# A last dense layer with low-rank adapters: split products and a masked adapter, or eight adapted weights and full-precision column halves

## What is computed

```python
x = x + einsum('bct,bcd->bdt', x, w0[cond])                   # mixing of the tokens, weight by batch
x = x + attention(x, block_table, kv_len)                     # 8 heads, 4 groups, window of 256, paged keys and values
x = x + einsum('bsi,bio->bso', x, W2[id]) + b2[id][:, None]   # one of 16 experts for each batch
H = einsum('btd,od->bto', x, W3)
delta = einsum('btr,bor->bto', einsum('btd,brd->btr', x, A[ad]), Bm[ad]) * scalings[ad]
x = x + H + delta                                             # ad: one of 8 adapters of rank 16 for each batch
```

## Time and profile before

| what | value |
|---|---|
| median of 3 runs | 1131.41 us (1126.84 to 1134.06) |
| profiled execution | 1129.37 us, span 1127.5 us, mean granted clock 0.969 |
| TensorE busy | 1043.9 us, 93% |
| VectorE, ScalarE, POOL busy | 659.9, 538.4, 534.1 us |
| phase 1 ends | at about 285 us |
| DMA | 196.16 MB, mean 174 GB/s |

### The profile page before, as it was taken

How to read it: one execution, slowest core, us unless ns; L and a number is a source line. 1 busy time by engine, 2 the same in 40 slices (tenths; PEclk the granted TensorE clock), 3 DMA queues, 4 the chain that set the end, 5 groups by cost and what they waited for, 6 DMA issues and landing times.

```text
span 1127.5 us, 23797 instructions
## 1 busy us (share of the span) xinstructions
PE 1043.9 (93%) x6418; PEld 704.5 (62%) x6418; DVE 659.9 (59%) x1928; ACT 538.4 (48%) x1337; POOL 534.1 (47%) x597
## 2 busy tenths in 40 slices
PE   7989999998579899999999999999999999999997
PEld 6767777676345566666666666666666666666655
DVE  5889896767345455555555555555554555555552
ACT  4457775674343444444444444444444444444440
POOL 3545444366555444545455545545454455454300
PEclk9999999999569899999999999999999999999998
DMA  4433443464367666575667666566765666566640
GB/s 131 143 117 135 150 153 116 161 194 139 92 180 209 178 186 200 184 218 178 181 193 219 207 187 211 185 185 181 220 209 182 187 214 186 175 201 214 194 147 20
DMA packets 95337, 196.16 MB, mean 174 GB/s; under 512 B 31346, under 2 KB 40114, under 8 KB 87110
## 3 DMA queue, kind: packets, MB, share of 16 engines
q1 hardware_dynamic: 63942, 149.49, 41.3%
q0 software_dynamic: 30784, 44.16, 14.3%
q10 hardware_dynamic: 576, 2.10, 0.5%
HBM read 195.08 MB, written 33.56 MB: 203 GB/s over the span
## 4 chain that ended last, share of the span: by engine, by line
PE 64%; issue 4%; ACT 3%; DMA 1%; another core or an unknown queue 1%; POOL 1%; DVE 1%; ACTq 0%; POOLq 0%; DVEq 0%
PE bank L93 23%; PE bank L1467 10%; PE bank L1442 9%; PE bank L1429 8%; PE bank L1421 8%; PE bank L1408 4%; PE bank L1398 2%; ACT PT L1227 2%; ACT KT L1227 1%; DMA KV<-kv_scratch,idxs 1%; DMA KV<-in_pool,idxs 1%; POOL KV L1129 0%; POOL KVE L1139 0%; DVE XB L1327 0%
## 5 line engine op out<-in xcount | busy, mean ns | idle before, releaser
L1227 ACT ACTIVATE PT<-bank 112x384 f32<-112x384 f32 x256 | 113.4, 489 | 254.4 <-PE bank L1429 211.6
L1305 DVE CUSTOM_DVE_ANT_0 SM<-bank,FM 128x336 f32<-128x336 f32 x256 | 129.7, 507 | 161.2 <-PE bank L1421 137.2
L1139 POOL DMA_INDIRECT KV<-kv_scratch,idxs x96 | 95.7, 997 | 127.2 <-DMA KV<-in_pool,idxs 103.9
L1139 POOL DMA_INDIRECT KVE<-kv_scratch,idxs_e x93 | 93.4, 1004 | 127.2 <-DMA KVE<-in_pool,idxs_e 102.5
L1236 ACT ACTIVATE PR<-SM,nb 128x336 f32<-128x336 f32 x256 | 145.5, 575 | 2.2 <-DVE nb L1309 2.1
L1129 POOL DMA_INDIRECT KV<-in_pool,idxs x96 | 95.1, 991 | 66.9 <-PE bank L1442 43.3
L1467 PE MATMUL bank<-W,XT 128*64 128x512 f32 x512 | 125.4, 612 | 0.7 <-ACT XT L1227 0.7
L1421 PE MATMUL bank<-KT,QB 64*128 64x336 f32 x512 | 111.2, 512 | 15.6 <-ACT KT L1227 8.8
L1227 ACT ACTIVATE KT<-bank 128x336 f32<-128x336 f32 x128 | 57.6, 450 | 141.2 <-PE bank L1408 134.8
L1129 POOL DMA_INDIRECT KVE<-in_pool,idxs_e x90 | 88.9, 988 | 70.8 <-PE bank L1442 42.7
L93 PE MATMUL bank<-wqh,XTH 128*128 128x512 f32 x256 | 105.2, 411 | 9.2 <-DVE XTL L500 5.8
(11 more groups left out here) (193 smaller groups left out, 2155.2 us busy)
## 6 DMA issues: line engine op xcount, KB each, us to landing
W<-in_w SPq DMA_DIRECT2D x64, 1024.0 KB
FM<-mask SPq DMA_DIRECT2D x64, 168.0 KB
X<-in_x SPq DMA_DIRECT2D x32, 256.0 KB
x_scratch<-X SPq DMA_DIRECT2D x32, 256.0 KB, 2.0
qt_scratch<-QT SPq DMA_DIRECT2D x32, 256.0 KB
QB<-qt_scratch SPq DMA_DIRECT2D x32, 256.0 KB
XB<-x_scratch SPq DMA_DIRECT2D x32, 256.0 KB
BB<-in_b SPq DMA_DIRECT2D x64, 128.0 KB
```

Source lines behind the costliest of these rows:

```text
L1139: pool.indirect_dma_start(out=KV[k][:, c, :], out_offset=None, in_=kv_d, in_offset=bass.IndirectOffsetOnAxis(ap=idxs[k][:, NCH + c:NCH + c ...
L1227: return nc.scalar.activation(dst, src, ACT.Copy)
L1305: v.tensor_tensor_reduce(out=SM[u % 2][:, :], in0=bank[u % 2][:, 0:SPAN], in1=FM[k][:, :], scale=1.0, scalar=-3e38, op0=ALU.add, op1=ALU.m ...
```

## The change

The eight possible weights of the last layer, W3 + scaling x (A Bm), are formed once and stay in SBUF (`W3E`, 128 x 16384 fp32). The last layer becomes eight fp32 matmuls of 64 stationary columns by 512, as the expert's are; the first batch of a pair reads its weight in W3E by an address from a register, the second reads a copy in `w3` that VectorE makes (`picked`). The split of the activations, the rank product and its mask go. On VectorE two slices are copied behind XO in front of `masked(pr, 4)`, two behind the bias addition in front of `masked(pr, 6)`.

- Forming: 32 steps (adapter, slice), each one float32r matmul with 48 contraction rows (high, low and high rows of A against high, high and low rows of Bm), to banks 6 and 7 in turn, and one VectorE scalar_tensor_tensor. 24 steps (`folded`, `products`) stand in pair 0 in eight places of three, on VectorE behind masked 1, masked 3, norm 1, masked 5, norm 2, masked 7 and two behind norm 3; 8 stand in pair 1 in two places of four.
- Late loads: W3 after pair 18 straight to `w3`, Wo after 23, A after 24, Bm after 27, the last two as 128 x 2048; six pieces of 1024 columns are split in place of five.
- XO lies over the phase 1 tile QT, XBB over XB3; VectorE waits in front of phase 2 for W3 and the last query store.

```diff
                 def late_low(i):
                     def run():
+                        part = slice(i % 2 * 1024, (i % 2 + 1) * 1024)
                         dve.wait_ge(s_wlh, i + 1)
-                        part = slice(i * 1024, (i + 1) * 1024)
-                        split(wlh[:, part], wll[:, part], wlr[:, part]).then_inc(s_wl, 1)
+                        if i < 2:
+                            split(woh[:, part], wol[:, part], wlr[:, part]).then_inc(s_wl, 1)
+                            return
+                        mixed, raw, neg = ((la, wlr[:, NWO:2 * NWO], nega), (lb, braw, negb))[i // 2 - 1]
+                        v.scalar_tensor_tensor(mixed[:, part], mixed[:, part].bitcast(F32), neg[:, 0:1], raw[:, part],
+                                               ALU.mult, ALU.add).then_inc(s_wl, 1)
...
-                                31: in_turn(late_low(3), late_low(4))})
+                                31: in_turn(late_low(3), late_low(4), late_low(5))})
...
+                    18: dense_weights, 23: output_weights, 24: adapter_inputs, 27: adapter_outputs})
...
                     if adapted:
                         act.wait_ge(s_x3p, at(r, 1, 0))
-                        copy(XTH3[:, :, :].rearrange("p k t -> p (k t)"), bank[7][:, :]).then_inc(s_xt3h, 1)
+                        copy(XT3[:, :, :, :].rearrange("p k b t -> p (k b t)"), bank[7][:, :]).then_inc(s_xt3, 1)
...
+                def adapted_weights(a, b):
+                    for i in range(a, b):
+                        ad, k = FOLDS[i]
+                        dve.wait_ge(s_low, i + 1)
+                        v.scalar_tensor_tensor(W3E[:, i * D:(i + 1) * D], bank[6 + i % 2][:, :], scb[:, ad:ad + 1],
+                                               w3[:, k, :], ALU.mult, ALU.add).then_inc(s_w3, 1)
+                def picked(q, ad, a, b):
+                    wait(dve, s_l3, q)
+                    for k in range(a, b):
+                        v.tensor_copy(w3[:, k, :], W3E[:, bass.ds(ad * (KC * D) + k * D, D)]).then_inc(s_w3c, 1)
...
                     if attention:
                         masked(pr, 0)
                         masked(pr, 1)
-                    if adapted:
-                        dve.wait_ge(s_xt3h, at(r, 1, 0))
-                        low(XTL3[:, :, :].rearrange("p k t -> p (k t)"), bank[7][:, :],
-                            XTH3[:, :, :].rearrange("p k t -> p (k t)")).then_inc(s_xt3, 1)
+                    if isinstance(p, int) and p == 1:
+                        adapted_weights(24, 24 + 4)
+                    folded(pr, 0)
...
+                        v.tensor_tensor(XO, bank[6][:, :], XB3[:, :], ALU.add).then_inc(s_xo, 1)
+                    if dense:
+                        ad = dve.value_load(aid[0:1, bass.ds(q * 2 + 1, 1)], min_val=0, max_val=NA - 1)
+                        picked(q, ad, 0, 2)
...
+                        v.tensor_tensor(XB3[:, :], XB2[:, :], BB[:, :], ALU.add).then_inc(s_xbb, 1)
+                        picked(q, ad, 2, KC)
 
                     if attention:
                         masked(pr, 6)
...
+                def dense3(r, ad, a, b):
+                    for k in range(a, b):
+                        pe.wait_ge(s_w3c, at(r, KC, k))
+                        for half in range(2):
+                            weight = w3[:, k, :] if half else W3E[:, bass.ds(ad * (KC * D) + k * D, D)]
+                            last = mm(bank[6][half * T:(half + 1) * T, :], XT3[:, k, half, :], weight,
+                                      start=(k == 0), stop=(k == KC - 1), skip_group_check=True)
+                    return last
+                def adapter_products(a, b):
+                    for i in range(a, b):
+                        ad, k = FOLDS[i]
+                        rows, g = slice(ad % 2 * T, ad % 2 * T + 3 * RANK), ad // 2 * D
+                        wait(pe, s_w3, i - 1)
+                        mm(bank[6 + i % 2][:, :], la[rows, g + k * P:g + (k + 1) * P], lb[rows, g:g + D], start=True,
+                           stop=True).then_inc(s_low, 1)
...
+                    if isinstance(p, int) and p == 1:
+                        adapter_products(24, 24 + 4)
                     if adapted:
+                        ad = pe.value_load(aid[0:1, bass.ds(r * 2, 1)], min_val=0, max_val=NA - 1)
                         pe.wait_ge(s_xt3, at(r, 1, 0))
-                        exact_products(mm, bank[7][:, 0:P], [(a_h[:, k, :], a_l[:, k, :], *x3t[k]) for k in range(KC)],
-                                       True, True).then_inc(s_xa, 1)
-                        dense3(0, 2, True)
+                        dense3(r, ad, 0, 2)
                     if attention:
                         scores(pr, 1)
+                        products(pr, 1)
                         turn(p, 0)
                         turn(p, 1)
+                    if isinstance(p, int) and p == 1:
+                        adapter_products(24 + 4, N_FOLDS)
+                        pe.wait_ge(s_w3, N_FOLDS)
                     if adapted:
-                        dense3(2, KC, False)
-                        pe.wait_ge(s_xal, at(r, 1, 0))
-                        exact_products(mm, bank[6][:, :], [(XAH[:, :], XAL[:, :], b_h[:, 0, :], b_l[:, 0, :])],
-                                       False, True).then_inc(s_l3, 1)
+                        dense3(r, ad, 2, KC).then_inc(s_l3, 1)
```

156 lines of the change are left out of this document (85 added, 71 removed).

## The result

The changed kernel takes 1146.86 us (median; 1141.51 to 1149.74), the kernel before 1132.74 on the same chip: ratio 1.0129, 95% interval 1.0081 to 1.0178. It is 1.3% slower, which is under 2% but clear of 1 by its interval; I had forecast 1114 us, a gain. The profiled execution took 1149.74 us, its span is 1147.9.

The account below looks back on a forecast made before the run. TensorE, busy 93% of the span, was taken as the bound; -49.0 + 18.6 + 0.5 + 14.5 - 2.5 = -17.9 us against the profiled 1129.37 gave 1111.5, 1114 us as a median, range 1088 to 1140.

Parts of the forecast that it names:

- TensorE's products: Steady loop: 5.18 us of products replaced by eight halves at 3.60, -1.58 us a pair, -49.0 us over 31 pairs.
- The register read: Steady loop: TensorE's read of the adapter number costs 0.6 us a pair, +18.6 us; bounds 0 and +38.
- A: Rival on the steady loop: register read hidden behind value products and dispatch lead, 1095 us; chance 0.25.
- C: Rival on the steady loop: TensorE also stops for address arithmetic before each register-addressed product, 1163 us; chance 0.17.
- Copies and VectorE: Steady loop: VectorE's four copies, 2.0 us a pair, fit its idle time and count nothing; uncovered, up to 31 us.
- Rival D: Steady loop: VectorE's SBUF copies hold up GpSimd's twelve gathers a pair, about 1245 us; chance 0.03.
- Phase change and first pairs: Late loads +0.5 us; forming in pairs 0 and 1 +14.5: pair 0 +6, pair 1 +7, lower clock +1.5.
- Tail: Last pair: eight halves at the lower clock replace 27 products, -2.5 us; bounds -1.7 and -5.3.
- The clock: Steady loop: granted clock taken to stay at its upper level, as TensorE's load hardly falls.
- The step that failed: Steady loop: GpSimd waits 2.8 us a pair for TensorE, so gathers could follow a period down to about 21.8 us.

Follow-up runs that it names:

- e1: Changed kernel with fixed adapter numbers, so no register reads on TensorE and VectorE, copies kept: 1149.45 us, ratio 1.0174 to the kernel before.
- e2: Changed kernel with fixed adapters and without VectorE's four copies a pair, both halves reading the formed weights directly: 1143.57 us, ratio 1.0098.
- e3: Changed kernel with the four copies and their register read moved from VectorE to ScalarE: 1140.03 us, ratio 1.0106.
- e4: Kernel before with four unused 128x512 copies a pair added on VectorE, in the change's places: 1129.25 us, ratio 0.996.
- e15: Kernel before with the gather order and three GpSimd zero fills a pair of e14, nothing of the change: 1101.66 us, ratio 0.9935.
- e17: e14 run again, beside the changed kernel on one chip: 1086.76 us, ratio 0.9822.
- e5: Changed kernel with three idle TensorE products a pair added, putting back about 1.2 us: 1140.57 us, ratio 1.0045.
- e9: Changed kernel with two of GpSimd's twelve gathers a pair left out from pair 4 on: 1101.75 us, ratio 0.9724.
- e11: Changed kernel with the second batch's old-row gathers put before the first batch's new-row gathers, nine in a row: 1278.38 us, ratio 1.1285.
- e12: Kernel before with the same gather reordering as e11 and nothing else: 1255.95 us, ratio 1.1077.
- e18: Changed kernel in e11's gather order, all three zero fills only in every second pair, one fill in the others: 1215.39 us, ratio 1.0733.
- e16: The changed kernel as it is, run on the same chip as e15 and e17: 1118.57 us, ratio 1.0085.
- e14: Changed kernel in e11's gather order with three GpSimd zero fills a pair, at most three gathers in a row: 1088.13 us, ratio 0.9812.
- e10: Changed kernel with the first batch's old-row gathers held back until TensorE's last-quarter scores: 1175.95 us, ratio 1.0382.

## Why the prediction was wrong

Point by point, by its own steps:

- **TensorE's products**, -1.58 us a pair: right. Without register reads (e1, e2) the shortest pair is 24.35 - 22.79 = 1.56 us shorter.
- **The register read**, +0.6: its direction was right, its size not; 0.35 us (e1). Beside the Trainium skill's floor of about 600 ns for a tensor load ("DMA: Bandwidth & Descriptors", section "Latency and other measured facts"), this trace shows a cost of 0.35 us and a gap of 0.18; how much of the read is hidden, it doesn't show. The measured value lies between A's nothing and mine, nearer to mine; C is refuted: no gap between the halves.
- **Copies and VectorE**, nothing: right (e2, e3, e4). Rival D did not happen: of some 300 gathers of the changed kernel between 450 and 1090 us 31 were stretched, to 1.24 us at most, and taking the copies away (e2) gave no time back. But my reason against it was weak. The scalings stretch no gather, the copies do: 26 gathers of e4 over 1.05 us, none in the kernel before, 5 in e2 without copies. The two aren't of one kind, either: 397 ns for 336 columns, 422 for 512. And its price held all twelve gathers where a pair has four copies. The rule of the Trainium skill's "SBUF — State Buffer", section "Who interferes with whom", is seen only as that stretch.
- **Phase change and first pairs**, +15.0: pair 4 begins 16.5 us later, but the nearness is luck. Pairs 2 and 3 give 3.3 us back, of the kind that I had counted in the loop. Pair 0 costs 14.9 us (from 27.5 to 42.4) where I had 6: hardly any of the 8 us that I let the waits take back came back, and pair 1's first scores are at 334.74, not near 325. Pair 1 costs 4.4 (25.1 to 29.5), not 7. On kind B, between e15 and e17, the start costs 24.0, above my bound of 22. The changed kernel's pairs 0 and 1 are as long there (42.4 and 29.6 us); what is shorter is the other kernel's start, 94.2 us for the first four pairs against 108.7. That start of the kernel before (kind A) has 15.8 us of unexplained waits of ScalarE and VectorE in it, e15 none; but e15 has another order of gathers too, so chip and order aren't told apart.
- **Tail**, -2.5: too small. From the start of the last pair's turn of activations to XO it took 10.36 us and takes 5.12, so -5.2, just inside the bound of -5.3: the eight halves run at the upper clock, in 3.65 us.
- **The clock**, left as it was: wrong by up to 12 us (the estimate above), as the six longest quarters each have it at the lower level.
- **The step that failed** stands in the first part: "So the gathers could follow a period down to about 21.8 us". I had subtracted GpSimd's mean wait for TensorE, 2.8 us a pair, from the period and taken the rest as fixed, for every pair alike. It isn't. The landings in the chain vary: in the changed kernel on kind A a wait for one is 3.4 us in the mean (175.1 / 51) but up to 5.1, against 3.2 and up to 4.2 before. So in 13 of 52 places GpSimd went on from new to old rows without a wait for TensorE between them, 10 of them late in the pair; in the kernel before in 4, none of them late. On kind A, gathers that TensorE's wait no longer parts then stand six in a row, ScalarE and VectorE stop until the run is over, and the clock falls. On kind B GpSimd never waits for TensorE before its old rows: the chain sets the period, 24.5 us.

Without that, 1127.5 + 16.5 - 31.2 - 8.4 = 1104 us would be the span; it is 1147.9, and the 43 us between are pairs 4 to 30 at 659.9 instead of 616.5. The next bound lay at the old period (24.5 us on kind B, against 24.35), not 2.5 us under it. I had given 0.19 to a slower kernel, but by C and D, and neither happened.

Shown: that the stalls come with the pace (e5), with GpSimd's gathers (e9) and with unbroken runs of them (e11, e12, e18), and that on kind B the chain decides without any stop (e16). Not shown: why a run of gathers stops other engines, why only on some chips (nine in a row were not tried on kind B), how long a break must be, how the 43 us divide between late gathers, stops and clock, and whether e14 beats the kernel before on kind A.

## What to carry to other kernels

When an engine's slack is read from its waits, ask what its other waits are made of: a wait for a transfer moves with the traffic, so "period less idle time" is no lower bound on a chain of issue and landing; add up the chain and price each landing at the busiest time it can meet. And an idle engine costs more than its idle time where the granted clock falls: look at the clock in the pairs that are long. Before shortening the busiest engine, give the next chain its slack first: here three fills and another order of the gathers took the changed kernel from 1118.57 to 1086.76 us on one kind of chip, the kernel before only from 1109.16 to 1101.66 (how much of this is the order's and how much the fills', no run tells). And try a change on more than one chip: the same kernel stood under two different bounds.

## What the runs showed of the hardware that I had not expected

- On chips of kind A, while gathers issued by GpSimd 1.3 us apart go on without a break, instructions of ScalarE and VectorE that have their inputs can wait until 0.5 to 1.7 us after the run: with nine in a row, ScalarE is idle for 8.65 us and VectorE for about 6 in nearly every pair (e11, at least 4.6 us of it with the inputs there); with six, ScalarE for up to 4.5 us (pair 18 of the changed kernel); with three, for up to 3.3 (e10). On kind B six in a row did nothing of the kind (e16).
- A fill of 128x1200 on GpSimd, 1.1 us, breaks a run of nine (e18), though a copy of 112x6, 0.2 us, doesn't (e11).
- Another sign of the kinds: SyncE's second mask issue starts 2.1 us or more behind the first in 22 of 25 pairs of the kernel before and in 23 of 25 of the changed one (kind A), and 1.4 us behind it in 25 of 26 pairs of e16 (kind B).
- After a stop with TensorE idle for 3.77 us the granted clock is 0.50 from before 792.4 to 799.1 us, and the expert's eight products take 3.68 us instead of 1.94 (pair 18).
- A chip's kind moves this kernel by 2% (1133 and 1109 us), more than the change does (1.3%).
- When TensorE got 1.2 us more to do in each pair (e5), the profiled loop became 18 us shorter, the median time 6.
